# A gated mixture layer's opening: the first two tiles multiplied centred and scaled afterwards, three of the four context matrices loaded later

## The chip, the cores and the metric

The kernel runs on one core of one Trainium2 chip. The metric is device time in microseconds (us) of one execution. A core has five engines with queues of their own that meet only through semaphores: TensorE (matmuls and transposes into PSUM), ScalarE, VectorE, GpSimd and SyncE. In the rows of the profile they are PE (PEld for its weight loads), ACT, DVE, POOL and SP; a "q" behind a name is the engine's sequencer, which issues transfers.

## The reference, cut to what matters

2048 tokens of 512 numbers pass two layers. The first is the one that the change touches:

```
h   = (x - mean(x)) / sqrt(var(x) + 1e-5)            # one token, 512 numbers
e   = min(clip(id, 0, 24999) // 6250, 3)             # the token's expert, 0 to 3
p   = h @ ctx[e].T
x1  = x + tanh(g_xattn) * ((silu(p) * p) @ ctx[e])
```

The second normalises x1 and runs a mixture of 16 experts with two chosen for each token and one shared expert. With the inputs drawn, 108 tokens belong to expert 0, 119 to expert 1, 131 to expert 2 and 1690 to expert 3, since three quarters of the identifiers are clipped.

## The kernel before, in words

**Tiles.** The kernel sorts the tokens by expert and cuts them into tiles of 128 rows, so 1, 1, 2 and 14 tiles for experts 0 to 3, with one spare: 19 tiles (NT). Tile 0 needs context 0, tile 1 context 1, tiles 2 and 3 context 2, the others context 3. The expert of a tile is read from `tile_e` at run time.

**Precision.** A product in float32 accuracy is made of three fp32r matmuls (`product`, L1311 to 1315): each operand is split in a high part (a copy rounded to fp32r) and a low part (the rest). So every context needs `ctx_hi` and `ctx_lo`, 128 x 2048 each, and every tile needs its transposed rows `hT` and its gated rows `gT` in both parts. A product with a whole context is 4 x 3 = 12 matmuls of 512 columns.

**One tile's way.** GpSimd gathers 128 rows of x (`gather_xa`, L419). VectorE takes mean and variance (`bn_stats`, `bn_aggr`) and works out the inverse root by a chain of one-column instructions (`roots`, L905). ScalarE writes the normalised rows `h` (`norm`, L574). TensorE transposes them (`transpose4`, psT[0]); ScalarE takes the high part, VectorE the low part (`low_h`). TensorE multiplies with the context into psG[0]; ScalarE applies silu, VectorE multiplies (`gate1`, into `gu`); TensorE transposes `gu` into psT[1], high and low parts are taken (`low_g`), and TensorE multiplies with the context again into psY[0]. VectorE adds the residual (`x1`, L972).

**Order.** Each engine has a written-out list. `stage1` calls `step(t, ...)` of each engine for t = -2 to 20; in it different tiles are at different places: in TensorE's step t (L1369) come the transposes of gu of tile t-1, the product of tile t, the transposes of h of tile t+1 and the second product of tile t-1. `have(known, k)` says whether tile t+k exists. A wait at the head of an engine's list holds everything behind it on that engine.

**The opening.** SyncE issues the constants and contexts 0, 1 and 2 at the start (L365 to 368), then waits for the rows of tile 2 and issues context 3, into `xh_sb` (L370). ScalarE makes the high part of each context (`high_ctx`, L552). The low parts come in two ways. For contexts 0 and 2 TensorE subtracts: per quarter one matmul of the raw context with the identity and one of the high part with minus the identity (`rest`, L1337 to 1345), and ScalarE copies the quarter out of PSUM (`take_rest`). For contexts 1 and 3 VectorE subtracts (`low_ctx`, L826). `ctx_lo_done` counts finished low parts in the order of the contexts; TensorE waits for it, at the expert's number plus one, ahead of each first product (L1372).

Of the kernel before, what the change touches and what calls it, by code (L numbers as in the profile page):

```python
# [27 lines left out]
ALU = mybir.AluOpType  # L28
# [50 lines left out]
def gated_layer(nc, x, ids, ctx_t, gates, w13, w2, gate_b, const, out):  # L79
    stack = ExitStack()  # L80
    with stack:  # L81
# [93 lines left out]
        sums = sb("sums", [P, 2, 2])  # L175
        nwt = sb("nwt", [P, 5, 2])
# [51 lines left out]
        minus_ready, rest_ps, rest_taken = sem("minus_ready"), sem("rest_ps"), sem("rest_taken")  # L228
        first_out = sem("first_out")
# [78 lines left out]
        def stage1(eng, step):  # L308

            for t in range(FIRST, LAST):  # L310
                step(t, t % 2, t)

        def columns_normed(t):

            return sum((0 <= n + 2 < NT and n != 0) + (n == FIRST + 1 or 0 <= n - 2 < NT) for n in range(FIRST, t + 1))
# [20 lines left out]
        def ctx_raw(e):  # L336

            if e < 2:
                return raw_flat[:, e * KD * D:(e + 1) * KD * D]
            return (ht if e == 2 else xh_sb)[:, :, :].rearrange("p a d -> p (a d)")  # L340
# [16 lines left out]
        def _(sp):  # L357
# [48 lines left out]
        def _(pool):  # L406
# [133 lines left out]
        def _(act):  # L540
# [15 lines left out]
            def take_rest(e, i):  # L556

                act.wait_ge(rest_ps, e // 2 * KD + i + 1)
                if e and i == KD - 1:

                    act.wait_ge(ctx_lo_done, 2)
                o = (e * KD + i) * D
                act.activation(ctx_lo[:, o:o + D], psG[i][:, :],  # L563
                               ACT.Copy).then_inc(rest_taken if i < KD - 1 else ctx_lo_done, 1)

            high_ctx(0)
            high_ctx(1)
            take_rest(0, 0)
            take_rest(0, 1)
            high_ctx(2)  # L570
            take_rest(0, 2)
            take_rest(0, 3)

            def norm(dst, src, col, done):  # L574
                act.activation(dst, src, ACT.Identity, scale=nwt[:, 3, col:col + 1],  # L575
                               bias=nwt[:, 4, col:col + 1]).then_inc(done, 1)

            def step(t, par, known):
# [7 lines left out]
                if known == 1:  # L586
                    high_ctx(3)
# [9 lines left out]
                if have(known, 0):  # L597
                    act.wait_ge(p_ps, t + 1)
                    if had(known, 0):
                        act.wait_ge(gu_ready, t)  # L600
                    act.activation(s_sb[:, 0:D], psG[0][:, :], ACT.Silu).then_inc(s_ready, 1)
                if have(known, 1):
                    act.wait_ge(hT_ps, t + 2)
                    act.activation(hT[0], psT[0][:, :], ACT.Copy).then_inc(hT_hi, 1)
                if known == -1:
                    take_rest(2, 1)
                    take_rest(2, 2)
                if known == 0:
                    take_rest(2, 3)
                if have(known, 2):  # L610
                    act.wait_ge(norm_ready, columns_normed(t) - (1 if have(known, -2) else 0))
                    if had(known, 1):
                        act.wait_ge(hT_ps, t + 1)
                    norm(h[:, par, :], xa_of(t, par, known), 1 if known == 0 else 0, h_ready)
                if known == FIRST:
                    take_rest(2, 0)
# [181 lines left out]
        def _(dve):  # L798
# [27 lines left out]
            def low_ctx(e, part, parts):  # L826

                dve.wait_ge(ctx_hi_done, e + 1)
                n = KD * D // parts
                c = slice(e * KD * D + part * n, e * KD * D + (part + 1) * n)  # L830
                return dve.tensor_tensor(ctx_lo[:, c], ctx_raw(e)[:, part * n:(part + 1) * n], as_f32(ctx_hi[:, c]),
                                         ALU.subtract)


# [70 lines left out]
            def roots(t, par, known, one, two, pair):  # L905

                base = NEWTON * columns_normed(t - 1)
                cols = ([0] if one else []) + ([1] if two or pair else [])
                done = [0]

                def each(op, last=False):
                    n = len(cols)
                    for i, col in enumerate(cols):
# [3 lines left out]
                        ins.then_inc(norm_ready if last else newton, 1)  # L917
# [21 lines left out]

                def offset(col, V, Y, T, R, B):  # L940
# [8 lines left out]
                if pair:  # L949
                    low_h(t, known)  # L950
                each(square)
                each(third)
                if had(known, 2):
# [4 lines left out]
                each(offset, last=True)  # L958

            def low_h(t, known):  # L960
                dve.wait_ge(hT_hi, t + 2)
                dve.tensor_tensor(hT[1], psT[0][:, :], as_f32(hT[0]), ALU.subtract).then_inc(hT_lo, 1)

            def step(t, par, known):
                one, two = have(known, 2) and known != 0, have(known, -2)
# [8 lines left out]
                def low_g():  # L974
                    if have(known, -1):
                        dve.wait_ge(gT_hi, t)
# [687 lines left out]
```

## Time and profile before

| | us |
|---|---|
| median of three runs | 477.3 (476.99 to 478.29) |
| the profiled execution, its own time | 476.73 |
| its span, first to last instruction | 474.9 |
| TensorE busy | 458.2 (96%) |
| VectorE busy | 316.9 (67%) |
| ScalarE busy | 268.1 (56%) |
| GpSimd busy | 212.5 (45%) |

The span is read from the first instruction to the last. The chain that ended last is followed back from the last instruction, at each step to what released it; what lies on the chain sets the time. The timeline gives start, duration, engine, line, operation and operands of each instruction (merged where alike), and in brackets the idle time before it. Matmuls overlap: a matmul's own duration is longer than the distance to the next one, and the chain shows the distance.

### The profile page before, as it was taken

To read this page: it belongs to the slowest core of one execution; us is meant where nothing else is said; L and a number is where in the kernel's file an instruction comes from. 1 tells how busy PE (TensorE), PEld (TensorE's weight loads), DVE (VectorE), ACT (ScalarE), POOL (GpSimd) and SP (SyncE) were. 2 spreads that over 40 slices of the span, in tenths; PEclk is the share of its full clock that TensorE was granted. 3 is DMA by queue.
4 is the path that set the end of the run, shared out by engine and by line. 5 is a ranking of instruction groups with operands and counts; after the bars stand their busy time and mean duration, and the time that the engine had idled before them with its cause. 6 is when DMAs were issued, how large, how long until landed. Compare 5 with 4: busy or idle time off the path is not lost.

```text
span 474.9 us, 7916 instructions
## 1 busy us (share of the span) xinstructions
PE 458.2 (96%) x2493; PEld 393.2 (83%) x2493; DVE 316.9 (67%) x789; ACT 268.1 (56%) x417; POOL 212.5 (45%) x175
## 2 busy tenths in 40 slices
PE   2999999999999999999999999999999999999993
PEld 1478888888888888888889999999999999999982
DVE  6679888878876554479469776566666676666520
ACT  4766556666564643633345676566655577656431
POOL 0513444664543475426168354443435455443242
PEclk9999999999999999999999999999999999999998
DMA  8643874776664542254289999889879998888555
GB/s 297 196 171 126 267 262 165 235 257 205 241 209 151 179 155 95 55 68 63 35 230 172 284 307 270 252 272 287 268 197 262 247 274 273 266 245 223 110 63 72
DMA packets 29166, 95.04 MB, mean 200 GB/s; under 512 B 4816, under 2 KB 5328, under 8 KB 28624
## 3 DMA queue, kind: packets, MB, share of 16 engines
q0 software_dynamic: 17040, 43.66, 37.4%
q1 hardware_dynamic: 11808, 50.98, 32.1%
q8 instruction: 17, 0.28, 0.2%
q14 instruction: 13, 0.11, 0.1%
q10 hardware_dynamic: 288, 0.01, 0.0%
HBM read 67.50 MB, written 28.70 MB: 203 GB/s over the span
## 4 chain that ended last, share of the span: by engine, by line
PE 95%; ACT 1%; DVE 1%; DMA 1%; POOLq 0%; POOL 0%; issue 0%
PE psG L1314 51%; PE psY L1314 32%; PE psT L1319 8%; PE psG L1572 1%; PE psG L1343 1%; DMA tok_i<-in_ids 1%; PE psY L1331 1%; ACT arena L563 0%; POOLq L81 0%; ACT arena L554 0%; PE psY L1450 0%; PE psG L1344 0%; POOL out L513 0%; PE psY L1476 0%; PE psG L1319 0%
## 5 line engine op out<-in xcount | busy, mean ns | idle before, releaser
L1314 PE MATMUL psY<-arena 128*128 (+1 forms) x372 | 90.8, 394 | 0.0
L1314 PEld LDWEIGHTS psY<-arena 128*128 128x128 f32 x372 | 68.7, 188 | 14.1 <-issue 0.2
L504 POOL DMA_INDIRECT ht<-out,idx x32 | 33.7, 1052 | 59.0 <-PE psT L1319 43.2
L1314 PE MATMUL psY<-slot,arena 128*128 128x512 f32 x240 | 58.8, 394 | 0.0
L1089 DVE TENSOR_TENSOR slot<-raw,slot 128x1536 fp32r<-128x1536 f32 x25 | 43.9, 1757 | 19.5 <-ACT slot L635 19.5
L1314 PE MATMUL psG<-arena 128*128 x228 | 56.8, 398 | 0.0
L1089 DVE TENSOR_TENSOR arena<-raw,arena 128x1536 fp32r<-128x1536 f32 x24 | 42.0, 1758 | 16.4 <-ACT arena L635 16.3
L1314 PEld LDWEIGHTS psY<-slot,arena 128*128 128x128 f32 x240 | 44.2, 188 | 9.2 <-ACT xh_sb L679 0.3
L1314 PE MATMUL psG<-arena,slot 128*128 128x512 f32 x216 | 51.3, 392 | 0.0
L1314 PEld LDWEIGHTS psG<-arena 128*128 128x128 f32 x228 | 41.5, 188 | 8.3 <-issue 0.4
L750 ACT ACTIVATE s_sb<-psG 128x224 f32<-128x224 f32 (+1 forms) x48 | 17.6, 366 | 54.6 <-PE psG L1314 54.6
L1314 PEld LDWEIGHTS psG<-arena,slot 128*128 128x128 f32 x216 | 40.1, 188 | 8.2
L513 POOL DMA_INDIRECT out<-ys,idx x16 | 32.3, 2017 | 32.1 <-DMA out<-xb,idx 17.9
L513 POOL DMA_INDIRECT out<-xb,idx x16 | 30.1, 1881 | 36.7 <-ACT xb L739 18.6
L437 POOL DMA_INDIRECT out<-xh_sb,idx x19 | 19.3, 1014 | 54.4 <-ACT xh_sb L575 54.4
L1314 PE MATMUL psG<-bl,slot 128*128 128x256 f32 (+1 forms) x264 | 42.1, 314 | 0.0
L1314 PE MATMUL psG<-slot,bl 128*128 128x448 f32 x192 | 40.3, 365 | 0.0
L1314 PE MATMUL psG<-arena,bl 128*128 128x448 f32 x192 | 40.3, 365 | 0.0
L1314 PEld LDWEIGHTS psG<-bl,slot 128*128 128x128 f32 x264 | 37.3, 189 | 3.0
L490 POOL DMA_INDIRECT out<-xh_sb,idxc x16 | 28.0, 1752 | 26.2 <-ACT xh_sb L679 24.4
L1314 PEld LDWEIGHTS psG<-slot,bl 128*128 128x128 f32 x192 | 36.0, 188 | 3.3
L1314 PEld LDWEIGHTS psG<-arena,bl 128*128 128x128 f32 x192 | 36.0, 188 | 3.3
(231 smaller groups left out, 814.6 us busy)
## 6 DMA issues: line engine op xcount, KB each, us to landing
raw<-in_w SPq DMA_DIRECT2D x51, 768.0 KB, 5.9
padded<-xh_sb SPq DMA_DIRECT2D x19, 256.0 KB, 2.3
raw<-in_ctx_t SPq DMA_DIRECT2D x2, 1024.0 KB, 8.7
ht<-in_ctx_t SPq DMA_DIRECT2D x1, 1024.0 KB, 11.7
xh_sb<-in_ctx_t SPq DMA_DIRECT2D x1, 1024.0 KB, 7.1
out<-log_sb SPq DMA_DIRECT2D x4, 256.0 KB, 7.6
ht<-out,idx POOLq DMA_INDIRECT x32, 5.2
xb<-in_x,idx POOLq DMA_INDIRECT x19, 3.8
```

The lines of the kernel that those rows point to most:

```text
L437: pool.indirect_dma_start(out, rows_of(t, 1), xh_sb[:, t % 2, :], None, bounds_check=TOK - 1, oob_is_err=False).then_inc(xh_sent[t % 2], 16)
L490: pool.indirect_dma_start(halves_of_out, ranked(1, j), y2[j % 4], None, compute_op=ALU.add).then_inc(y2_sent[j % 4], 16)
L504: pool.indirect_dma_start(ht[:, n, :], None, halves_of_out, slots(e * NA + a, 0)).then_inc(g_here[n], 16)
L513: pool.indirect_dma_start(halves_of_out, slots(e * NA + a, 1), y3[e % 2][:, a, :], None, compute_op=ALU.add).then_inc(added[a], 16)
L750: act.activation(dst, src, ACT.Silu).then_inc(silu3, 1)
L1089: dve.tensor_tensor(piece(SLOT[r][1], c), raw[:, c, :], as_f32(piece(SLOT[r][0], c)), ALU.subtract).then_inc(w_lo[c], 1)
L1314: ins = pe.matmul(ps, left[a], right[b], start=n == 0 and m == 0, stop=n == total - 1 and m == 2)
L1319: ins = pe.transpose(ps[:, k * P:(k + 1) * P], src[:, k * P:(k + 1) * P], ident)
L1331: ins = pe.matmul(psY[1][:, 0:2 * NT], onehot1[:, j, :], q_tok[0][:, j, 0:2 * NT], start=j == 0, stop=j == NJ - 1)
L1343: pe.matmul(psG[i][:, :], ident, ctx_raw(e)[:, s], start=True, stop=False)
L1572: ins = pe.transpose(psG[3][:, o:o + P], gu[:, s:s + P], ident)
```

## The change

It concerns the first microseconds of the first layer.

- SyncE issues context 0 at the start, then contexts 1, 2 and 3, each after the rows of tile 0, 1 and 2 have landed; context 3 also waits for context 0's low part, whose raw space in `raw` it takes over (it lay in `xh_sb`).
- TensorE subtracts the low part of context 0 alone. The low parts of contexts 1, 2 and 3 are subtracted by GpSimd, each as one instruction over 128 x 2048. The first two stand ahead of the gathers of tiles 4 and 5 in GpSimd's queue, the third behind them.
- Tiles 0 and 1 are not normalised: VectorE subtracts the mean (one `tensor_scalar` over 128 x 512 each), and the root is applied after the product, as the scale of silu and of the gating (`r01`). Tile 1 has `hT1` in `bl0` and its product in psG[1].
- The steps -2, -1 and 0 of every engine are replaced by written-out lists; the loop begins at t = 1.

The core of the diff:

```diff
 SyncE
-            for e in range(E1 - 1):
+            for e in range(E1):
+                if e:
+                    sp.wait_ge(xa_here[e - 1], 16)
+                if e == E1 - 1:
+                    sp.wait_ge(ctx_lo_done, 1)
                 sp.dma_start(ctx_raw(e), ctx_t[e, :, :]).then_inc(ctx_here[e], 16)
-            sp.wait_ge(xa_here[2], 16)
-            sp.dma_start(ctx_raw(E1 - 1), ctx_t[E1 - 1, :, :]).then_inc(ctx_here[E1 - 1], 16)
 GpSimd
+            def low_ctx(e):
+                pool.wait_ge(ctx_hi_done, e + 1)
+                pool.wait_ge(ctx_lo_done, e)
+                c = slice(e * KD * D, (e + 1) * KD * D)
+                pool.tensor_tensor(ctx_lo[:, c], ctx_raw(e), as_f32(ctx_hi[:, c]), ALU.subtract).then_inc(ctx_lo_done, 1)
+            low_ctx(1)
+            low_ctx(2)
             gather_xa(4)
             gather_xa(5)
+            low_ctx(3)
 ScalarE
+            high_ctx(0)
+            for i in range(KD):
+                take_rest(i)
+            hT_high(0)
+            high_ctx(1)
+            hT_high(1)
+            silu1(0)
+            high_ctx(2)
+            norm_h(2)
             def step(t, par, known):
...
                 if have(known, 0):
+                    silu1(t)
                 if have(known, 1):
+                    hT_high(t + 1)
                 if have(known, 2):
+                    norm_h(t + 2)
+                if known == 1:
+                    high_ctx(3)
 VectorE
+            for t in range(2):
+                stats_of(t)
+                mean_of(t, t)
+                dve.tensor_scalar(h[:, t, :], xa[:, t, :], mv[:, t, 0:1], None, ALU.subtract).then_inc(h_ready, 1)
+            low_h(0)
+            roots(-1, 1, -1, False, False, True)
+            low_h(1)
+            stats_of(2)
+            gate1(0)
+            mean_of(2, 0)
+            roots(0, 0, 0, True, False, False)
             def step(t, par, known):
...
+                if known == 1:
+                    gate1(t)
+                    low_g(t - 1)
+                    low_h(t + 1)
                 if one:
+                    stats_of(t + 2)
 TensorE
-            rest(2, 0)
+            pe.wait_ge(h_ready, 1)
+            transpose4(psT[0], h[:, 0, :]).then_inc(hT_ps, 1)
+            w = context_of(0)
+            pe.wait_ge(hT_lo, 1)
+            inner(0, w, range(KD // 2))
+            pe.wait_ge(h_ready, 2)
+            transpose4(psT[0], h[:, 1, :]).then_inc(hT_ps, 1)
+            inner(0, w, range(KD // 2, KD)).then_inc(p_ps, 1)
+            w = context_of(1)
+            pe.wait_ge(hT_lo, 2)
+            inner(1, w, range(KD)).then_inc(p_ps, 1)
             def step(t, par, known):
```

`context_of(t)` reads the tile's expert and waits for `ctx_lo_done`; `inner(t, w, ks)` is the first product over the quarters `ks`; `hT_high`, `silu1`, `norm_h`, `low_h`, `low_g`, `gate1`, `stats_of` and `mean_of` are the operations of before under names. `silu1` and `gate1` take `r01` as a factor for tiles 0 and 1.

## Rows read from the trace of the kernel before

**Rows 1.** The page, busy time by engine, and the granted clock in 40 slices.
```profile
PE 458.2 (96%) x2493; PEld 393.2 (83%) x2493; DVE 316.9 (67%) x789; ACT 268.1 (56%) x417; POOL 212.5 (45%) x175
...
PEclk9999999999999999999999999999999999999998
```

**Rows 2.** The chain that ended last, in order of time: start us, us, what.
```profile
13.52 0.43 PE psG L1344
...
23.62 2.77 PE psG L1314 x12
...
26.82 0.86 PE psG L1343 x2
27.68 0.23 PE psG L1344
...
28.52 3.00 PE psG L1314 x12
...
31.95 2.78 PE psY L1314 x12
34.73 0.44 PE psT L1319 x4
35.16 2.78 PE psG L1314 x12
...
466.38 0.70 ACT xb L739
```

**Rows 3.** Timeline of TensorE, 5 to 21 us: start us, us, engine, line, operation.
```profile
12.53 1.41 PE L1344 MATMUL psG<-arena,minus 128*128 128x512 f32 x1
...
16.75 0.79 PE L1344 MATMUL psG<-arena,minus 128*128 128x512 f32 x1
...
20.82 0.63 PE L1319 MATMUL psT<-cst,front 128*128 128x128 f32 x4 [0.90 <-ACT arena L563]
```

**Rows 4.** Timeline of SyncE.
```profile
18.72 0.33 SPq L371 DMA_DIRECT2D xh_sb<-in_ctx_t  x1
```

**Rows 5.** Landing times of the context transfers: issues, KB each, median us.
```profile
raw<-in_ctx_t SPq DMA_DIRECT2D x2, 1024.0 KB, 8.7
...
xh_sb<-in_ctx_t SPq DMA_DIRECT2D x1, 1024.0 KB, 7.1
```

**Rows 6.** Landing times of all 51 weight loads of 768 KB (line 363).
```profile
DMA to landing us min/median/max: 4.2/5.9/8.9
```

**Rows 7.** Timeline of GpSimd.
```profile
0.75 0.53 POOL L407 MEMSET log_sb<- 128x512 f32 x1 [0.29 <-POOLq L1658]
...
12.36 1.15 POOL L425 DMA_INDIRECT front<-in_x,idx  x1 [11.09 <-DVE idx L883]
```

**Rows 8.** Timeline of ScalarE.
```profile
11.86 1.91 ACT L554 ACTIVATE arena<-raw 128x2048 fp32r<-128x2048 f32 x1 [0.53 <-DMA raw<-in_ctx_t]
...
18.41 1.08 ACT L563 ACTIVATE arena<-psG 128x512 fp32r<-128x512 f32 x2
...
26.43 0.60 ACT L601 ACTIVATE s_sb<-psG 128x512 f32<-128x512 f32 x1 [1.46 <-PE psG L1314]
26.92 0.59 ACT L604 ACTIVATE arena<-psT 128x512 fp32r<-128x512 f32 x1
```

**Rows 9.** Timeline of VectorE.
```profile
16.05 0.69 DVE L993 BATCH_NORM_STATS2 stats<-front 128x6 f32<-128x512 f32 x1 [2.62 <-DMA front<-in_x,idx]
...
22.12 0.69 DVE L962 TENSOR_TENSOR arena<-psT,arena 128x512 fp32r<-128x512 f32 x1 [0.93 <-ACT arena L604]
...
23.58 2.29 DVE L831 TENSOR_TENSOR arena<-raw,arena 128x2048 fp32r<-128x2048 f32 x1
27.05 0.69 DVE L983 TENSOR_TENSOR gu<-s_sb,psG 128x512 f32<-128x512 f32 x1 [1.18 <-ACT s_sb L601]
...
30.38 0.17 DVE L1007 BATCH_NORM_AGGREGATE mv<-stats 128x2 f32<-128x6 f32 x1
...
32.12 0.16 DVE L943 SCALAR_TENSOR_TENSOR nwt<-mv,nwt 128x1 f32<-128x1 f32 x1
```

More of the change, by code:

```diff
@@ L308, in stage1, with hT_of, p_bank @@
         def stage1(eng, step):
-            for t in range(FIRST, LAST):
+            for t in range(1, LAST):
                 step(t, t % 2, t)
+        hT1 = [bl0[:, n * KD * P:(n + 1) * KD * P] for n in range(2)]
+        def hT_of(t):
+            return hT1 if t == 1 else hT
+        def p_bank(t):
+            return psG[1 if t == 1 else 0][:, :]
         def columns_normed(t):
-            return sum((0 <= n + 2 < NT and n != 0) + (n == FIRST + 1 or 0 <= n - 2 < NT) for n in range(FIRST, t + 1))
+            return sum((n + 2 < NT) + (0 <= n - 2 < NT) for n in range(t + 1))
         def have(known, k):
@@ L824, in along @@
                 return ap.unsqueeze(1).to_broadcast([P, n, ap.shape[1]])
[L826 to L832, printed above, removed]
             dve.memset(tot[:, 0:1], 0.0)
@@ L905, in roots, with each @@
             def roots(t, par, known, one, two, pair):
-                base = NEWTON * columns_normed(t - 1)
-                cols = ([0] if one else []) + ([1] if two or pair else [])
+                base = 0 if pair else 2 * (NEWTON - 1) + NEWTON * columns_normed(t - 1)
+                cols = [0, 1] if pair else ([0] if one else []) + ([1] if two else [])
                 done = [0]
-                def each(op, last=False):
+                def each(op, last=None):
                     n = len(cols)
@@ L948, in roots @@
                 each(second)
-                if pair:
-                    low_h(t, known)
                 each(square)
                 each(third)
-                if had(known, 2):
+                if pair:
+                    each(root01, last=r01_ready)
+                    return
+                if known and had(known, 2):
                     dve.wait_ge(h_ready, t + 2)
@@ L1367, in transposed, with context_of, inner @@
                 transpose4(row_bank(j), row_tile(j)).then_inc(bT_ps, 1)
+            def context_of(t):
+                w = weights(t)
+                pe.wait_ge(ctx_lo_done, pe.snap(w + 1))
+                return w
+            def inner(t, w, ks):
+                hi, lo = hT_of(t)
+                for k in ks:
+                    s = slice(k * P, (k + 1) * P)
+                    ins = product(p_bank(t), [hi[:, s], lo[:, s]], ctx(w, k), k, KD)
+                return ins
+            pe.wait_ge(h_ready, 1)
[9 more added lines that the diff above has]
+            inner(1, w, range(KD)).then_inc(p_ps, 1)
             def step(t, par, known):
-                if have(known, 0):
-                    w = weights(t)
-                    pe.wait_ge(ctx_lo_done, pe.snap(w + 1))
+                if have(known, 0) and known != 1:
+                    w = context_of(t)
                 if have(known, -1):
@@ L1388, in step @@
                     half_up(0, 1)
[L1389 removed]
+                if have(known, 0) and known != 1:
                     pe.wait_ge(hT_lo, t + 1)
[L1391 to L1394 removed]
+                    inner(t, w, range(KD)).then_inc(p_ps, 1)
                 if have(known, 1) and known < 3:
                     h_transposed()
[L1397 to L1401 removed]
                 if ROWS0 <= known < ROWS0 + TB:
```

180 lines of the change are left out of this document (71 added, 109 removed).

## The prediction

> **What bounds the kernel now.** I read the page first: TensorE is busy 96% of the span and the other engines at most 67% [rows 1]. Then the chain of waits in order of time. From 23.62 us, where the first product with context 0 starts, to the last copy at 466.38 the chain is TensorE almost without a break [rows 2]. So after 23.6 us nothing but TensorE's queue sets the end: whatever delays that queue moves the end by as much, and nothing behind it can absorb the delay. The change touches only what lies before about 45 us, so I compare one mark in both kernels: the start of the second product of tile 0 (psY), now at 31.95 [rows 2]. From there both kernels issue the same matmuls in the same order. The timelines of the engines give the durations. The profiled execution took 476.73 us; the sum is made against that. The median of the runs shown is 477.3.
>
> **What the change gives.** Context 2's low part leaves TensorE: four quarters, each 0.86 + 0.23 us on the chain [rows 2], 4.4 us in all, one of them behind the first product. The chain of inverse roots leaves the way to tile 0's first transpose: TensorE is done with context 0's quarters before 18.9 us (ScalarE copies the last two out from 18.41 to 19.49 [rows 8]) and transposes the centred rows at once instead of at 20.82 [rows 3]; ScalarE's copy of them (0.6) follows its last quarter, VectorE's low part takes 0.69 [rows 9], and the first product starts near 20.8 instead of 23.6. Centring is one pass over 128 x 512. No row shows it; I take 0.6 us, a little under the statistics on the same tile (0.69 [rows 9]), and between 0.3 and 0.7 it ends before ScalarE's copy does, so it costs nothing unless tile 1's rows land after 18.2 us. The root as a scale of silu costs nothing extra; in the gating at most 0.1 us. Issuing contexts 1 and 2 late empties the queue for context 0, but its quarters wait for the sorting matmuls ahead of them on TensorE anyway: nothing gained.
>
> **What the change costs.** Tile 1 belongs to expert 1, so its first product waits for both parts of context 1. This is the new chain:
>
> 1. Tile 0's rows land at 16.05, when VectorE's statistics start on them [rows 9]. Only then is context 1 issued. SyncE answers at once, and a transfer of this size, issued after tile rows in the same way and beside the same gathers, took 7.1 us [rows 4, 5]: 23.2. Bounds: 4.9 (the fastest of the 768 KB loads took 4.2 [rows 6]; a third more bytes would make it 5.6 if all of it went with the size, and I stay between) and 8.7 [rows 5].
> 2. High part on ScalarE, 1.91 us [rows 8]: 25.1.
> 3. Low part on GpSimd. No row shows this operation. From below, four times a fill of 512 columns, 4 x 0.53 = 2.1 us [rows 7], about VectorE's 2.29 for the same subtraction [rows 9]; from above three such streams one after the other, 6.4. I take 4.3, two streams, since the operation has two operands to read where the fill has none: 29.4. The Trainium skill, "GPSIMD Engine Reference", section 3.1, gives 4.50 us for GpSimd and 2.29 for VectorE on a tensor_tensor of 2048 float32 columns; the trace agrees on VectorE's, and no run here shows GpSimd's. With it this sum would be 0.2 longer.
> 4. The product of tile 1, 2.8 us [rows 2]: 32.2, where it was over at 31.5 before. TensorE has stood idle from 24.0 (20.8, two halves of the product and a transpose, 3.2 us) to 29.4.
> 5. Now the order bites. The transposes of tile 0's gated rows stand behind the product in TensorE's list; and in VectorE's step 1 the gating of tile 1 stands ahead of tile 0's low part, and it needs ScalarE's silu, which stands behind the copy of gu. So in series: transposes 0.6 [rows 3], copy 0.5, silu 0.6 [rows 8], gating 0.6, low part 0.7 [rows 9]: the second product of tile 0 starts at 35.2. Before it had started at 31.95, because its low part was taken beside tile 1's product. So +3.25 us. The normalised rows of tile 2 are transposed in this gap.
> 6. Context 3's high part (1.91) stands on ScalarE behind the normalisation of tile 3, which ends near 39.1 (low part of tile 2 to 35.8, statistics and roots 2.6 by the distance from 30.38 to 32.28 and the 0.69 before it, rows 9; normalisation 0.8). It ends at 41.0; behind it wait the copy of tile 1's gated rows and VectorE's low part of it, done at 42.2, when TensorE has been free for the second product since 41.6. So +0.6.
>
> What is hidden: GpSimd's second low part, 29.4 to 33.7, holds the gathers of tiles 4 and 5; tile 4's rows land near 38, where VectorE wants them at 39. A gather slow by 3 us would cost a few tenths. The third, about 41 to 45.3, is done ahead of tile 4's product (about 52), and the residual rows gathered behind it land before their use at 51. The high part of context 2 stands ahead of tile 2's normalisation, which is over at about 29. Sum so far: 3.25 + 0.6 = +3.9, 480.6 us.
>
> 7. TensorE's clock. The granted clock reads 1.00 in every slice [rows 1], the 2.4 GHz level, and yet the same matmul takes 1.41 us at 12.53 and 0.79 at 16.75 [rows 3]; on the chain 0.43 and 0.23 apart [rows 2]. So after the idle start TensorE works at half speed, as at 1.2 GHz, until some 5 us of dense work have gone by, whatever the record says. A pause of 0.9 us (before 20.82 [rows 3]) did not bring that back. The new pause is 5.4 us. Its price lies between 0 and the whole product of tile 1 at half speed, 12 x (0.43 - 0.23) = 2.4 us; a second product at that level would double it. I take 2.4, since the pause is far longer than the harmless one and the opening needed longer than this product to get fast: 483.0 us. The Trainium skill, "TensorE: Matmul & The Clock Gate", Part 1, says the same of idle stretches, that the array falls to half its clock and regains it only under sustained work; the trace's opening agrees with the second half, and no pause in this trace tests the first.
>
> The three runs lie from 476.99 to 478.29, mostly above the profiled execution, so I put the forecast at 483.2.
>
> **Rivals.**
> - *The clock stays up.* Steps 1 to 6 hold, step 7 costs nothing: 480.9. For it: the record shows no fall at all, and if context 1 lands a microsecond earlier the pause is short. Against it: the slow matmuls at the start, under the same record.
> - *The leg to context 1 is short* and the change is faster. The price of steps 1 and 3 together is 11.4 us in my sum; the gain from tile 0's early start is only kept where they take under 7.5. With 4.9 and 2.1 they take 7.0, the hold-up on ScalarE (0.6) dissolves as well and tile 0's rows, gathered without contexts 1 and 2 on the way, land 0.4 sooner; the pause is under a microsecond then. 3.9 - 4.4 - 0.6 - 0.4 = -1.5 us: 475.5. Against it: both ends at once, with six gathers beside the transfer.
> - *Even.* One end of the two (the transfer at 4.9 or GpSimd at VectorE's rate) and the other half way, no fall of the clock: about 477.5.
> - *The opening is hidden.* If TensorE had slack later, nothing would show: 477.3. The unbroken chain speaks against it [rows 2]; I count it with the even case.
>
> **How the numbers follow.** Waits with a slower clock 0.50, waits without 0.37, even 0.06, faster 0.07. A measurement here tells about 0.3%, 1.4 us. The range reaches from the second case with a transfer of 4.9 us (3.9 - 2.2 = +1.7, so 478.6) to the forecast with one of 8.7 and a little more on GpSimd (+1.6 + 1.3, so 486.1). That leaves out the even and the faster case and the far ends.
>
> **What would show it.** Right: in the changed trace the first product starts near 20.8 in two halves; TensorE then idles about 5 us, ended by GpSimd's subtraction; that instruction takes over 4 us; context 1 takes about 7 us to land; psY's first product starts after 35 us; the product of tile 1 takes over 4 us instead of 2.8. Wrong: context 1 landing before 21.5 or a subtraction under 3 us, then the second product starts before 32; or TensorE pausing elsewhere after 45 us, which would point at the gathers behind GpSimd's work. If tile 1's matmuls lie 0.23 apart, the clock stayed.

## The result and the profile after

The changed kernel takes 487.85 us (median of six runs, 486.73 to 489.31) against 477.08 for the kernel before (six runs, 475.91 to 478.29): 1.0228 times as long, 95% interval 1.0211 to 1.0245. It is slower by 10.8 us. The forecast was 483.2 with a range up to 486.1: the direction was right, the size was too small. Of all runs in this document one, of f1 at 581.4 us, was in a slower state; its median counts it, its ratio does not. The profiled execution of the changed kernel took 489.31 us with a span of 487.3; against the span of 474.9 before that is +12.4. It is the slowest of the six, and the one before lies a little under its median, so a part of these 12.4 us, 1.6, is the spread between executions.

The page, busy time of TensorE and the granted clock, answers to [rows 1]:

```profile
PE 458.0 (94%) x2481; PEld 393.8 (81%) x2481; DVE 322.6 (66%) x786; ACT 264.7 (54%) x411; POOL 222.5 (46%) x178
...
PEclk9979899999999999999999999999999999999998
```

TensorE is busy as long as before (458.0 against 458.2), although the four quarters of context 2 are gone: what they cost has come back, most of it as slower matmuls, and the 12.4 us of the span are idle time. The clock now falls below full speed in two early slices.

Where it was lost is seen by laying TensorE's timelines side by side (start us, us, engine, line, operation, tiles; in brackets the idle time before it and what ended it). First the kernel before:

```profile
23.46 2.93 PE L1314 MATMUL psG<-arena 128*128 x12
...
28.48 3.03 PE L1314 MATMUL psG<-arena 128*128 x12
...
31.71 3.02 PE L1314 MATMUL psY<-arena 128*128 x12
...
38.13 3.02 PE L1314 MATMUL psY<-arena 128*128 x12
...
41.78 3.00 PE L1314 MATMUL psG<-arena 128*128 x12
...
48.13 2.98 PE L1314 MATMUL psG<-arena 128*128 x12
```

These are the first products (psG) of tiles 0, 1, 3 and 4 and, between them, the second products (psY) of tiles 0 and 1; tile 2's lie in the gaps. The changed kernel, whose lines answer to these and to [rows 3]:

```profile
20.98 1.65 PE L1341 MATMUL psG<-arena 128*128 x6 [1.94 <-DVE arena L987]
...
29.59 4.82 PE L1341 MATMUL psG<-arena,bl 128*128 x12 [5.13 <-POOL arena L490]
...
35.77 0.66 PE L1346 MATMUL psT<-cst,front 128*128 128x128 f32 x4 [0.92 <-ACT front L589]
38.30 3.03 PE L1341 MATMUL psY<-arena 128*128 x12 [1.88 <-DVE arena L991]
...
45.39 3.01 PE L1341 MATMUL psY<-arena 128*128 x12 [0.41 <-DVE arena L991]
50.67 1.09 PE L1346 MATMUL psT<-cst,gu 128*128 128x128 f32 x4 [2.27 <-DVE gu L1001]
...
52.26 3.77 PE L1341 MATMUL psG<-arena 128*128 x12
...
59.38 2.98 PE L1341 MATMUL psG<-arena 128*128 x12
```

| start of | before | after | later by |
|---|---|---|---|
| first product, tile 0 | 23.46 | 20.98 | -2.48 |
| first product, tile 1 | 28.48 | 29.59 | 1.11 |
| second product, tile 0 | 31.71 | 38.30 | 6.59 |
| second product, tile 1 | 38.13 | 45.39 | 7.26 |
| first product, tile 3 | 41.78 | 52.26 | 10.48 |
| first product, tile 4 | 48.13 | 59.38 | 11.25 |
| end of the span | 474.9 | 487.3 | 12.4 |

Two steps of that table were forecast in size: tile 1's product, and, with the clock's 2.4, most of the second product of tile 0. One was not: 3.2 us between the second product of tile 1 and the first product of tile 3, with a wait of 2.27 us for `gu` of tile 2 in front of it. The cause is on VectorE. GpSimd's timeline, which answers to [rows 7], shows the three subtractions:

```profile
24.94 4.51 POOL L490 TENSOR_TENSOR arena<-raw,arena 128x2048 fp32r<-128x2048 f32 x1 [5.12 <-ACT arena L580]
29.71 4.56 POOL L490 TENSOR_TENSOR arena<-ht,arena 128x2048 fp32r<-128x2048 f32 x1 [0.26 <-ACT arena L580]
...
44.13 4.59 POOL L490 TENSOR_TENSOR arena<-raw,arena 128x2048 fp32r<-128x2048 f32 x1 [7.49 <-ACT arena L580]
```

and VectorE's, which answers to [rows 9], shows its own instructions beside them:

```profile
25.98 0.68 DVE L1011 BATCH_NORM_STATS2 stats<-ys 128x6 f32<-128x512 f32 x1
26.58 0.73 DVE L998 SCALAR_TENSOR_TENSOR gu<-psG,r,s_sb 128x512 f32<-128x512 f32 x1
...
27.81 1.66 DVE L949 SCALAR_TENSOR_TENSOR nwt<-nwt 128x1 f32<-128x1 f32 x1
29.50 0.16 DVE L952 SCALAR_TENSOR_TENSOR nwt<-nwt 128x1 f32<-128x1 f32 x1
29.70 4.59 DVE L949 SCALAR_TENSOR_TENSOR nwt<-nwt 128x1 f32<-128x1 f32 x1
...
40.06 0.22 DVE L949 SCALAR_TENSOR_TENSOR nwt<-nwt 128x1 f32<-128x1 f32 x1
...
45.75 3.12 DVE L949 SCALAR_TENSOR_TENSOR nwt<-nwt 128x1 f32<-128x1 f32 x2
...
49.84 0.69 DVE L1001 TENSOR_TENSOR gu<-s_sb,psG 128x512 f32<-128x512 f32 x1
```

One link of the inverse root (L949, one column, two inputs in SBUF) takes 0.22 us at 40.06, with GpSimd at rest. The one that starts at 27.81 ends at 29.47, the one at 29.70 ends at 34.29, and the pair at 45.75 ends at 48.87. GpSimd's subtractions end at 29.45, 34.27 and 48.72. So each such link lasts until GpSimd is done; the link at 29.50 falls between two subtractions and takes 0.16. Statistics over 512 columns at 25.98 (one SBUF input) and the gating at 26.58 (the same kind of instruction as the links, but with one input in SBUF and one in PSUM) ran beside the first subtraction at their usual 0.68 and 0.73: neither the length nor the kind of VectorE's instruction decides.

What the late roots hold up is seen in ScalarE's timeline (of [rows 8]), where the copy of tile 0's gated rows and silu of tile 1 stand behind the normalisation of tile 2:

```profile
34.91 0.81 ACT L589 ACTIVATE front<-ys,nwt 128x512 f32<-128x512 f32 x1 [5.28 <-DVE nwt L966]
35.63 0.58 ACT L624 ACTIVATE arena<-psT 128x512 fp32r<-128x512 f32 x1
36.10 0.68 ACT L602 ACTIVATE s_sb<-psG,r 128x512 f32<-128x512 f32 x1
```

So the chain that ended last, unbroken TensorE from 23.62 before [rows 2], now passes through these links (start us, us, what):

```profile
15.97 6.95 DMA raw<-in_ctx_t
...
27.81 1.67 DVE nwt L949
...
29.70 4.60 DVE nwt L949
...
45.78 3.09 DVE nwt L949 x2
...
172.66 4.47 DMA front<-padded,idxc
```

The first line is context 1's transfer, the last one a gather late in the first layer, which is taken up at the end.

The Trainium skill says the same of the links: in "GPSIMD Engine Reference", section 8 (Key points), GpSimd shares its SBUF interfaces with VectorE and collides with VectorE instructions that have two SBUF inputs; in "SBUF — State Buffer", section "SBUF: two separate sides", the shared pair is an exclusive lock that one instruction holds for its whole length while the other one stands. The links of 1.66, 4.59 and 3.12 us agree with it. The prediction read the first of these pages for GpSimd's duration and passed over this line.

The granted clock by stretches of 6 us and one of 4 (length; busy time of PE, PEld, DVE, ACT, POOL with counts; clock; DMA share; GB/s), in the changed kernel:

```profile
24.00:30.00 6.00, 0.87 (x4) 0.45 (x3) 4.46 (x9) 3.83 (x4) 4.80 (x2) 0.72 1.01 395
28.00:32.00 4.00, 2.41 (x6) 1.93 (x7) 3.93 (x3) 1.63 (x1) 3.74 (x2) 0.50 0.89 341
30.00:36.00 6.00, 5.08 (x18) 3.83 (x18) 4.77 (x4) 1.09 (x2) 5.55 (x3) 0.71 0.27 102
...
48.00:54.00 6.00, 3.73 (x14) 3.07 (x13) 5.94 (x27) 2.82 (x5) 3.07 (x4) 0.72 0.28 96
```

The 0.72 and 0.71 are means over both levels: in the four microseconds from 28 to 32 the clock reads 0.50, the 1.2 GHz level. It falls in the pause of 5.13 us, and again around the pause of 2.27 us. Tile 1's product lasts 4.82 us where the same twelve matmuls take 3.03 at full speed before, and tile 3's 3.77.

### The profile page after: what moved, and what is told of

Read it like the earlier page. It is cut to its first block, busy times and chain, and to the rows that moved or that the text cites. A ratio compares the mean times of both kernels' runs of the same rounds, so it can differ in the third digit from the quotient of the medians.

```text
span 487.3 us, 7886 instructions
## 1 busy us (share of the span) xinstructions
PE 458.0 (94%) x2481; PEld 393.8 (81%) x2481; DVE 322.6 (66%) x786; ACT 264.7 (54%) x411; POOL 222.5 (46%) x178
## 4 chain that ended last, share of the span: by engine, by line
PE 86%; DVE 6%; DMA 4%; issue 2%; ACT 1%; POOLq 0%; POOL 0%; DVEq 0%
PE psG L1341 46%; PE psY L1341 30%; PE psT L1346 6%; DVE nwt L949 2%; PE psG L1607 1%; DMA raw<-in_ctx_t 1%; DMA front<-padded,idxc 1%; DMA front<-in_x,idx 1%; DMA tok_i<-in_ids 1%; PE psY L1358 1%; DMA padded<-xh_sb 0%; POOLq L81 0%; POOL out L539 0%; PE psY L1511 0%; PE psG L1346 0%
## 5 line engine op out<-in xcount | busy, mean ns | idle before, releaser
L1341 PE MATMUL psG<-arena 128*128 x216 | 55.0, 403 | 1.9 <-DVE arena L987 1.9
L1341 PE MATMUL psG<-arena,bl 128*128 128x448 f32 (+1 forms) x204 | 45.1, 378 | 5.1 <-POOL arena L490 5.1
L1341 PEld LDWEIGHTS psG<-arena 128*128 128x128 f32 x216 | 39.8, 192 | 9.7 <-issue 2.2
L1341 PEld LDWEIGHTS psG<-arena,bl 128*128 128x128 f32 x204 | 39.6, 194 | 9.8 <-issue 5.6
L539 POOL DMA_INDIRECT out<-xb,idx x16 | 29.4, 1838 | 34.0 <-ACT xb L768 23.9
L539 POOL DMA_INDIRECT out<-ys,idx x16 | 29.9, 1869 | 30.8 <-ACT ys L768 22.0
```

The lines of the kernel that those rows point to most:

```text
L539: pool.indirect_dma_start(halves_of_out, slots(e * NA + a, 1), y3[e % 2][:, a, :], None, compute_op=ALU.add).then_inc(added[a], 16)
L1341: ins = pe.matmul(ps, left[a], right[b], start=n == 0 and m == 0, stop=n == total - 1 and m == 2)
```

## The experiments

The theories. **P:** GpSimd's subtraction stops VectorE's links with two SBUF inputs; these hold the normalisation of tile 2 and the gating of tile 2, and with them TensorE. **L:** what costs is the length of the leg to context 1 (transfer, high part, GpSimd) in front of tile 1's product. **C:** what costs is TensorE's clock, which falls in the pauses. All experiments are edits of the changed kernel; each ran beside the kernel before, at 477.03 to 477.28 us. A trace shows one execution, and where context 1 is issued after tile 0's rows its landing alone moves between 22.9 and 23.5 us, so half a microsecond between two traces can be chance.

**e1: all three low parts on VectorE, GpSimd subtracts nothing.** Context 1 ahead of `low_h(1)`, context 2 in step 1, context 3 in two halves in steps 2 and 3.

```diff
 GpSimd
-            low_ctx(1)
-            low_ctx(2)
             gather_xa(4)
             gather_xa(5)
-            low_ctx(3)
 VectorE
...
+            low_ctx(1).then_inc(ctx_lo_done, 1)
             low_h(1)
...
+                    low_ctx(2).then_inc(ctx_lo_done, 1)
...
+                if known == 2:
+                    link(low_ctx(3, 0, 2))
+                if known == 3:
+                    low_ctx(3, 1, 2).then_inc(ctx_lo_done, 1)
```

> The changed kernel with the three low parts subtracted by VectorE (2.29 us each, the third in two halves) and no arithmetic on GpSimd. Theory P (an instruction of VectorE with two SBUF tensor inputs stands still while GpSimd's subtraction runs): no link of the root chain (line 949 of the changed kernel) is longer than 0.3 us; the leg to context 1 gets 2.2 us shorter, the tensor engine's pause before tile 1's product about 3 us; the second product of tile 0 starts near 33.7 us instead of 38.3, the wait ahead of tile 2's gated rows (2.3 us) goes; 479 to 481 us. Rival L (only the lateness of context 1 counts, the long links are harmless): the 2.2 us of the leg and about 2 us of the clock, 483 to 484 us.

Measured: 486.69 us, 1.0199 (1.0179 to 1.0219). The links are back at 0.22 us, tile 1's product starts 1.26 us sooner, at 28.33, and yet nearly all of the gain is gone. TensorE's timeline shows why:

```profile
28.33 5.46 PE L1353 MATMUL psG<-arena,bl 128*128 x12 [3.84 <-DVE bl L993]
...
36.97 4.60 PE L1353 MATMUL psY<-arena 128*128 x12 [2.30 <-DVE arena L997]
```

Both products run at half speed or near it; the granted clock is 0.73, 0.70 and 0.72 in the three stretches from 24 to 42 us. So P's mechanism is absent here and C has eaten the gain. A miss for the size that P gave (479 to 481 us).

**e2: GpSimd subtracts in eight pieces of 256 columns.**

```diff
-                c = slice(e * KD * D, (e + 1) * KD * D)
-                pool.tensor_tensor(ctx_lo[:, c], ctx_raw(e), as_f32(ctx_hi[:, c]), ALU.subtract).then_inc(ctx_lo_done, 1)
+                n = KD * D // 8
+                for i in range(8):
+                    c = slice(e * KD * D + i * n, e * KD * D + (i + 1) * n)
+                    ins = pool.tensor_tensor(ctx_lo[:, c], ctx_raw(e)[:, i * n:(i + 1) * n], as_f32(ctx_hi[:, c]),
+                                             ALU.subtract)
+                ins.then_inc(ctx_lo_done, 1)
```

> The changed kernel with each of GpSimd's three subtractions cut in eight instructions of 256 columns; the work is the same. Theory P: VectorE gets in between the pieces, no link of the root chain is longer than 0.9 us (one piece is 4.5/8 = 0.56 us and some start), and the wait of the tensor engine for tile 2's gated rows goes; GpSimd's leg is 0 to 1 us longer; 484 to 486 us. Rival L: the links may shorten but the time does not fall, 487.5 to 489 us. Rival S (the long links come from something else than GpSimd's instruction, such as the semaphores): links of 1.7 to 4.6 us stay.

Measured: 490.06 us, 1.0263 (1.0244 to 1.0282). GpSimd's timeline has the first subtraction, VectorE's a pair of links beside the third:

```profile
25.50 5.52 POOL L492 TENSOR_TENSOR arena<-raw,arena 128x256 fp32r<-128x256 f32 x8 [5.49 <-ACT arena L584]
```

```profile
46.39 1.21 DVE L953 SCALAR_TENSOR_TENSOR nwt<-nwt 128x1 f32<-128x1 f32 x2
```

A link now lasts about as long as one piece (1.21 / 2 = 0.6 us; a piece takes 5.52 / 8 = 0.69). That is P's mechanism: the wait follows the length of GpSimd's instruction. The time was missed (484 to 486 us expected): the leg is 1.0 us longer (5.52 against 4.51), tile 1's product behind it takes 4.61 us, and beside the third subtraction more links wait, so that TensorE still waits 2.48 us for `gu` of tile 2.

**e3: the links of the root with one tensor input.** The second input is one column, so it can be given as the scalar of a `tensor_scalar`; GpSimd is left as it is.

```diff
-                    return dve.scalar_tensor_tensor(T, Y, V, Y, ALU.mult, ALU.mult)
+                    return dve.tensor_scalar(T, Y, V, Y, ALU.mult, ALU.mult)
...
-                    return dve.scalar_tensor_tensor(T, T, -10 / 3 * RS_W, T, ALU.add, ALU.mult)
+                    return dve.tensor_scalar(T, T, -10 / 3 * RS_W, T, ALU.add, ALU.mult)
...
```

> The changed kernel with the root chain written as tensor_scalar: the second tensor operand of each link (one column) becomes a per-partition scalar, so that each instruction has one tensor input. GpSimd is untouched. Theory P, that two tensor inputs are what clashes: all links at 0.15 to 0.35 us though GpSimd's subtraction runs; the copy of tile 0's gated rows is no longer held up, the second product of tile 0 starts near 37.3 instead of 38.3, the 2.3 us wait goes; 483.5 to 485.5 us. If any VectorE instruction of the chain clashes: links of 1.7 to 4.6 us stay and the time too, 487.5 to 488.5 us.

Measured: 486.71 us, 1.0205 (1.0181 to 1.0229). GpSimd subtracts from 25.48 to 29.99, and VectorE's link in the middle of it takes 0.27 us (its timeline, then TensorE's):

```profile
28.36 0.27 DVE L949 TENSOR_SCALAR nwt<-nwt 128x1 f32<-128x1 f32 x1
```

```profile
30.13 5.36 PE L1341 MATMUL psG<-arena,bl 128*128 x12 [4.58 <-POOL arena L490]
...
38.66 4.58 PE L1341 MATMUL psY<-arena 128*128 x12 [2.30 <-DVE arena L991]
```

So the collision needs the second tensor input; the same arithmetic with one is free of it. The wait of 2.27 us for `gu` of tile 2 is gone too. But the time, expected at 483.5 to 485.5, falls by only 1.1 us, which the intervals do not tell from nothing, since TensorE again has two pauses, and both products behind them run at about half speed (5.36 and 4.58 us). As in e1, C takes over.

**e4: context 1 issued at the start.** One edit on SyncE, so that the leg begins sooner.

```diff
-                if e:
+                if e >= 2:
                     sp.wait_ge(xa_here[e - 1], 16)
```

> The changed kernel with context 1 issued at the start behind context 0, as before the change. Rival L: tile 1's product starts near 26.3 us instead of 29.6, after a pause of 2 us and at full clock, the second product of tile 0 near 32; 481 to 482.5 us. Theory P: tile 1's product starts as early, but GpSimd's second subtraction (about 29.7 to 34.3) now meets the roots of tile 2, whose normalisation holds ScalarE; the second product of tile 0 starts near 36 to 37, and the third subtraction stops the chain again; 485 to 487 us.

Measured: 487.6 us, 1.0212 (1.0195 to 1.0229), as the changed kernel and a little above the 485 to 487 that P gave. That a shorter leg is enough, as L says, falls: the subtraction begins 2.56 us sooner and the time does not fall, because it now stops other links, those of the roots of tiles 0 and 1 (timelines of GpSimd and VectorE):

```profile
22.38 4.54 POOL L490 TENSOR_TENSOR arena<-raw,arena 128x2048 fp32r<-128x2048 f32 x1 [2.54 <-ACT arena L580]
```

```profile
22.42 4.59 DVE L961 SCALAR_TENSOR_TENSOR r<-nwt 128x1 f32<-128x1 f32 x2
```

VectorE's low part of tile 1 stands behind them, and TensorE waits 2.92 us for that, until 27.85.

**e5: VectorE's low part of tile 0 ahead of the gating of tile 1** in step 1, the order that the prediction's step 5 blamed.

```diff
                 if known == 1:
-                    gate1(t)
                     low_g(t - 1)
+                    gate1(t)
                     low_h(t + 1)
```

> The changed kernel with VectorE's step 1 in another order: the low part of tile 0's gated rows ahead of the gating of tile 1. The second product of tile 0 starts 1.3 us earlier (37.0). Since context 3's high part, and with it GpSimd's third subtraction, hang on other work, the wait ahead of tile 2's gated rows takes that gain back in part: 486.5 to 488 us.

Measured: 489.1 us, 1.0258 (1.0237 to 1.028): no gain, where 486.5 to 488 were expected. In the trace the second product of tile 0 starts at 38.01 instead of 38.30, and not at 37.0. TensorE's timeline, then ScalarE's:

```profile
30.18 5.48 PE L1341 MATMUL psG<-arena,bl 128*128 x12 [5.68 <-POOL arena L490]
```

```profile
36.55 0.60 ACT L624 ACTIVATE arena<-psT 128x512 fp32r<-128x512 f32 x1 [0.36 <-PE psT L1346]
```

Here tile 1's product started 0.6 us later than in the changed kernel's trace and took 5.48 us instead of 4.82, and ScalarE's copy waited for TensorE and no longer for the normalisation. In the old order the low part would have followed silu and gating, and the second product would have started near 39.2 (an estimate from their durations in the two traces). So the order is worth about 1.2 us at this place, but it does not reach the end: TensorE still waits 2.28 us for `gu` of tile 2, behind the roots that the third subtraction stops, until 51.02, where the changed kernel's wait ends at 50.67. The order is no cause of any size while the roots are late.

**e6: the pauses of TensorE filled with matmuls that nobody reads** (47 in all, into a free PSUM bank, in four pauses up to tile 3's product), everything else as in the changed kernel.

```diff
+            def busy(n):
+                for i in range(n):
+                    pe.matmul(psG[2][:, :], minus[:, :], ctx_hi[:, 0:D], start=True, stop=True)
+
+            busy(20)
             w = context_of(1)
             pe.wait_ge(hT_lo, 2)
...
```

> The changed kernel with matmuls that nobody reads (psG[2], 0.23 us each) put into the tensor engine's pauses: 20 ahead of tile 1's product, 11 ahead of the transposes of tile 2, 7 ahead of the second product of tile 0, 9 ahead of tile 2's gated rows. No wait is changed. Theory C (a part of the loss is the clock that falls in the pauses): the granted clock stays 1.00, tile 1's product takes 2.8 us instead of 4.7; but GpSimd's second subtraction still holds the roots of tile 2 and so ScalarE until 35.7 us, so the second product of tile 0 starts near 38.3 as before and only the later half-speed stretch (52 to 56 us) is gained: 485.5 to 486.5 us. If the clock were no cost: 487.5 to 489 us.

Measured: 487.86 us, 1.022 (1.0194 to 1.0247): a miss (485.5 to 486.5 expected). The clock stays at 1.00 in every stretch up to 60 us and tile 1's product takes 3.00 us instead of 4.82, but the second product of tile 0 is no sooner in TensorE's timeline:

```profile
29.99 3.00 PE L1341 MATMUL psG<-arena,bl 128*128 x12 [1.30 <-POOL arena L490]
...
38.63 3.01 PE L1341 MATMUL psY<-arena 128*128 x12
```

With the links still stopped, TensorE waits for VectorE whether its matmuls are fast or slow. By tile 4's product e6 is 1.05 us ahead of the changed kernel (58.33), since tile 3's is fast too; 0.63 us are lost again at 286.40, where TensorE waits behind a slow load of weights, so the traces do not rule out that the clock alone is worth some tenths.

**e7: both at once**, the one-input links of e3 and 21 + 9 matmuls in the two pauses that e3 has.

```diff
+            busy(21)
             w = context_of(1)
...
+                    if known == 1:
+                        busy(9)
                     pe.wait_ge(gT_lo, t)
...
```

> The kernel of e3_one_input (no clash with GpSimd) with such matmuls in its two pauses: 21 ahead of tile 1's product, 9 ahead of the second product of tile 0. With neither the clash nor the fallen clock only the waits of the prediction's steps 1 to 6 are left: the second product of tile 0 near 35.5 to 36.5 us, 480.5 to 483 us. If a third cause is at work: above 484 us.

Measured: 484.07 us, 1.0149 (1.0131 to 1.0167), above the 480.5 to 483 expected and at the edge of what was to point at a third cause. Now it shows in TensorE's timeline:

```profile
36.12 3.05 PE L1341 MATMUL psY<-arena 128*128 x12 [0.21 <-DVE arena L991]
...
47.48 3.03 PE L1341 MATMUL psG<-arena 128*128 x12
```

| median, us | clock as it comes | clock kept up |
|---|---|---|
| links with two inputs | 487.85 (the change) | 487.86 (e6) |
| links with one input | 486.71 (e3) | 484.07 (e7) |

Each cause alone is worth 1.1 or nothing, both together 3.8, and only the last is clear of the noise: each hides the other. At tile 4's product the traces say the same: against the changed kernel's 59.38 e3 is 2.75 us ahead, e6 1.05, and e7 5.51. What remains, 484.07 - 477.08 = 7.0, is waiting at full clock. 0.34 us of it is the price of the one-input links: one takes 0.27 us instead of 0.22, and at 167.61 TensorE waits 0.34 us behind a chain of them, a wait that f1 has too and f2, with two inputs there, has not.

**f1 to g2: can the opening be better than both kernels?** f1 takes the idea the other way round: contexts 0, 1 and 2 are issued at the start; context 1's low part is taken by VectorE before tile rows arrive (13.79 to 16.12); contexts 2 and 3 stay with GpSimd, behind the gathers of tiles 4 and 5; the roots have one input. Not shown below: TensorE waits for context 1's low part ahead of tile 0's product; ScalarE makes the high parts of contexts 1, 2 and 3 earlier in its list; VectorE's list has the low part of tile 0's gated rows ahead of the gating of tile 1, as in e5, and the gating of tile 0 behind the roots of tile 2.

```diff
 SyncE
-                if e:
-                    sp.wait_ge(xa_here[e - 1], 16)
                 if e == E1 - 1:
-                    sp.wait_ge(ctx_lo_done, 1)
+                    sp.wait_ge(xa_here[2], 16)
+                    sp.wait_ge(ctx_lo_done, 2)
 GpSimd
-            low_ctx(1)
-            low_ctx(2)
             gather_xa(4)
             gather_xa(5)
+            low_ctx(2)
             low_ctx(3)
 VectorE
+            dve.wait_ge(ctx_hi_done, 2)
+            dve.tensor_tensor(ctx_lo[:, KD * D:2 * KD * D], ctx_raw(1), as_f32(ctx_hi[:, KD * D:2 * KD * D]),
+                              ALU.subtract).then_inc(ctx_lo_done, 1)
             for t in range(2):
                 stats_of(t)
...
```

> The changed kernel's centred opening with the three causes removed: contexts 0, 1 and 2 issued at the start; context 1's low part on VectorE in its idle time before the rows of tile 0 land; contexts 2 and 3 on GpSimd behind the gathers, with roots of one tensor input; tile 0's low part ahead of the gating, context 3's high part ahead of a normalisation. Tile 1's product follows tile 0's at once (near 24.4 us), the second product of tile 0 starts near 29.1 instead of 31.95 before the change, no pause over 2 us, clock 1.00: 473.5 to 475.5 us, 2 to 4 us below the kernel before. If the early start is worth nothing: 477 us.

Measured: 478.07 us, 1.0008 (0.9982 to 1.0034), as the kernel before: a miss. TensorE paused 2.44 us ahead of tile 0's product and both halves were slow (2.02 and 2.55 us instead of 1.64). In f2 the low part of tile 0 stands ahead of tile 1's centring, and the roots of later tiles have two inputs again; f3 adds five unread matmuls. In the expectations from here on P stands for the order and the pause ahead of tile 0's product, R for transfers and C for the clock.

```diff
             for t in range(2):
                 stats_of(t)
+                if t:
+                    low_h(0)
                 mean_of(t, t)
...
-            low_h(0)
...
+                link = dve.tensor_scalar if known is not None and known < 3 else dve.scalar_tensor_tensor
```

> f1 with two edits: VectorE takes tile 0's low part ahead of tile 1's centring (f1 left TensorE 2.44 us without work ahead of tile 0's product), and the roots have one tensor input only up to step 2, while GpSimd subtracts; afterwards they are those of the kernel before, since the longer form cost 0.35 us on the chain at 158 to 160 us in f1. If the pause sets both the start and the clock (P): tile 0's product starts at 19.5 to 20.0 instead of 20.69 and its halves take 1.64 each instead of 2.02 and 2.55; psY of tile 0 at 28 to 29.5; tile 4's product at 45 to 46.5; 474 to 476.5 us. If the transfers of tile rows or context 3 come next (R): TensorE waits for them before 50 us, tile 4's product stays at 47, 477 to 478.

> f2 with 5 matmuls that nobody reads (1.1 us) in the remaining pause ahead of tile 0's product. If the clock falls in that pause too in f2, this one is 0.5 to 1.5 us faster than f2; if the pause of about 1.4 us is harmless, the two are the same within 0.5 us.

Measured: f2 476.51 us, 0.9986 (0.9971 to 1.0); f3 476.84 us, 0.9988 (0.9977 to 0.9998). The start that f2 was to have was not met: the low part had been put behind the statistics of tile 1, which waited for that tile's rows until 19.71, so tile 0's product started at 21.27, in f2 behind an even longer pause. In f3 the halves take 1.66 and 1.64 us, and its tile 4's product starts 0.87 us sooner (46.97 against 47.84), but its time is no better than f2's. g1 puts it ahead of them, and tile 1's low part ahead of tile 2's statistics; g2 adds the five matmuls.

```diff
             for t in range(2):
-                stats_of(t)
                 if t:
                     low_h(0)
+                stats_of(t)
...
-            stats_of(2)
-            mean_of(2, 0)
             low_h(1)
+            stats_of(2)
+            mean_of(2, 0)
```

> f2 left tile 0's low part behind the statistics of tile 1, and these waited for tile 1's rows until 19.71, so the product started at 21.27 after a pause of 3.07 us. Here the low part of tile 0 stands ahead of the statistics of tile 1, and tile 1's low part ahead of the statistics of tile 2. If that order was the cause (P): tile 0's product starts at 19.5 to 19.9 behind a pause of about 1.4 us, its halves take 1.64 each (the clock stays at 1.00), tile 1's product starts at 23.3 to 24.2, psY of tile 0 at 28 to 29.5, tile 4's product at 44.8 to 46.2; 474 to 475.8 us. If the clock falls after 1.4 us as well (C): halves of 2 us or more, psY of tile 0 near 30, 475.5 to 477.

> g1 with 5 matmuls that nobody reads (1.1 us) in the pause ahead of tile 0's product. By P the same as g1 within 0.5 us (the pause of 1.4 us costs no clock); by C 0.8 to 1.5 us faster than g1, with halves of 1.64 us here alone.

Measured: g1 476.07 us, 0.9971 (0.9959 to 0.9983); g2 476.33 us, 0.9984 (0.9975 to 0.9993). TensorE's timelines, first f2's, with the pause ahead of tile 0's product, then g1's:

```profile
21.27 2.46 PE L1342 MATMUL psG<-arena 128*128 x6 [3.07 <-DVE arena L984]
```

```profile
20.17 1.63 PE L1342 MATMUL psG<-arena 128*128 x6 [1.69 <-DVE arena L984]
...
29.53 3.03 PE L1342 MATMUL psY<-arena 128*128 x12 [1.06 <-DVE arena L988]
...
46.12 3.00 PE L1342 MATMUL psG<-arena 128*128 x12
...
164.61 0.66 PE L1347 MATMUL psT<-cst,front 128*128 128x128 f32 x4 [0.37 <-DMA front<-padded,idxc]
```

After 3.07 us the half product takes 2.46 us, after 1.69 us it takes 1.63, and g2's filled pause gains nothing more. g1 is the fastest kernel of this study, a little above the 474 to 475.8 us expected, 1.1 us under the kernel before and at the edge of what can be told. Since f1 to g2 change the leg and the order of three engines together, they show that these waits can be had back, and not which edit gives what. It is 2.0 us ahead at tile 4's product (46.12 against 48.13); about half of that is lost later, part of it at 164.61, where TensorE waits for a gather.

## Why the prediction was right in direction and wrong in size

The sum had 3.9 us of waits (steps 1 to 6), 2.4 us of clock (step 7), and nothing for what GpSimd's work does to VectorE. The runs split the 10.8 us into 7.0 of waits (e7) and 3.8 that the stopped links and the clock take together. So two places failed: "what is hidden", which was not hidden, and the waits of steps 5 and 6, which were sized too small.

- **Steps 1 to 4 held.** Context 1 was issued at 15.97 and landed at 22.94 (7.0 us, forecast 7.1), its high part took 1.91 us, GpSimd 4.51 us (forecast 4.3; the 4.50 that the prediction quotes from the Trainium skill, "GPSIMD Engine Reference", section 3.1, was nearer), and tile 1's product started at 29.59 (forecast 29.4). The first product started at 20.98 (forecast 20.8).
- **"What is hidden" is a step that failed.** It costed GpSimd's second and third subtraction at nothing because their results were early enough. Their results were; but while they ran, VectorE stood. The first one stopped a link of tile 2's roots for 1.66 us and the second one the next for 4.59, and tile 2's normalisation, "which is over at about 29", ended at 34.91 + 0.81 = 35.7; in e7, where no link is stopped, it ended at 31.0. The third one held the roots of later tiles with tile 2's gating behind them: TensorE waited 2.27 us, and 3.2 us were lost between the second product of tile 1 and the first of tile 3. Steps 1 to 7 came to 6.3 us for the whole change; 7.26 were lost by tile 1's second product, and this is what took it to 10.5. One of the prediction's own signs of being wrong came with it, TensorE pausing after 45 us (2.27 us before 50.67), though the cause was not the gathers that the sign was to point at.
- **Step 5 had nearly the right time for the wrong reason.** With step 7 it put the second product of tile 0 at 35.2 + 2.4 = 37.6; it started at 38.30. But the chain that it followed through silu was entered late: silu of tile 1 stood behind the normalisation of tile 2, not behind tile 1's product. That the time came out near is luck. The order that it blamed is worth about 1.2 us in e5's trace, by an estimate, and nothing in its time, since later roots take the gain back.
- **Step 7 had the mechanism, was mis-sized at its place and was counted only once.** Tile 1's product took 4.82 - 3.03 = 1.8 us longer, not 2.4. But the clock also fell around the pause of 2.27 us, where tile 3's product took 3.77 instead of 3.00, and this would have been worse without the stopped links: in e1 and e3 the second product of tile 0 ran at half speed as well (4.60 and 4.58 us). The Trainium skill, "TensorE: Matmul & The Clock Gate", Part 1, says that an idle array falls to half its clock; the 0.50 from 28 to 32 us, after the pause of 5.13 us, agrees.
- **The waits were sized too small even without both.** Steps 1 to 6 said +3.9; e7, with fast links and full clock, is 47.48 - 41.78 = 5.7 us late at tile 3's product and 7.0 us slower in the end. Steps 5 and 6 are part of it: the second product of tile 0 is 36.12 - 31.71 = 4.4 late, where step 5 said 3.25, and that of tile 1 43.52 - 38.13 = 5.4, where steps 5 and 6 said 3.85. Half a microsecond of the first comes from tile 1's product, which started at 29.91; silu and gating with the root as a factor took 0.68 and 0.75 us instead of 0.60 and 0.69, which the prediction put at nothing and at most 0.1. What comes behind tile 3's product is open but for the 0.34 us of the one-input links.
- **A part is open.** From tile 4's product (+11.25) to the end (+12.4) of the profiled execution another 1.1 us went. 0.42 of it, at 177.17, is TensorE's wait for the gather that the chain shows with 4.47 us. In the kernel before, and in e6, TensorE did not wait for that gather, which landed there in at most 3.5 us. Why it takes about a microsecond longer in some kernels, and where the rest went, was not tried.
- **The rivals.** "The clock stays up" at 480.9 (483.2 less step 7's 2.4 is 480.8) was refuted by the clock and would have been too low by e7's 484.07. "The leg to context 1 is short" did not occur, and e4 shows that a leg shorter by 2.56 us gives nothing here while GpSimd's work stops VectorE. The even and the hidden case, at 477.3 to 477.5, did not occur either.

## What to carry to other kernels

When work is moved to GpSimd, ask not only when its result is needed but which VectorE instructions run beside it: one with two inputs in SBUF, however small, may stand until GpSimd's instruction ends, and one link of a serial chain passes the whole wait on. Where the second input is a column, a `tensor_scalar` with a scalar from SBUF avoids it (0.27 us against 4.59, though 0.22 with GpSimd at rest). And test two suspected causes together as well as apart: here each alone showed a microsecond or nothing, and only both showed 3.8 us.

## What the runs showed of the hardware

- A VectorE instruction on one column with two SBUF inputs waited out GpSimd's whole instruction: 4.59 us beside 128 x 2048, about 0.6 us beside 128 x 256. With one SBUF input it was not touched (0.27 us beside GpSimd and without it), nor was the gating with one input in SBUF and one in PSUM (0.73).
- GpSimd's subtraction of 128 x 2048 float32 took 4.51 to 4.63 us, VectorE's 2.29; in eight pieces GpSimd needs 5.52, so a piece costs (5.52 - 4.51) / 7 = 0.14 us of its own.
- TensorE's speed fell after shorter pauses than expected: 2.13 us (e3), 2.44 us (f1) and 3.07 us (f2) ahead of tile 0's product were followed by a first half of 2.03, 2.02 and 2.46 us. But 2.42 us in e5 were followed by 1.64, as 1.69 us were in g1 (1.63): the length of the pause alone does not decide.
